# First feed-forward layer of an attention stack: second map in three fp32r passes on split operands, squares of the context rows on GpSimd, their sums spread out

## What is computed

```python
x = x + L0_xattn(layernorm(x), ctx_768, ...)
x = x + L0_ffn(layernorm(x), Wp, sim_matrix, temperature, W1, b1, W2, b2)
x = x + L1_xattn(layernorm(x), ctx_768, ...)
# L0_ffn: E = 8 experts, D = 128, F = 512
comb = top-2 gates of each token, zero for the other experts
h   = gelu(einsum('bsd,edf->ebsf', x, W1) + b1[:, None, None, :])
eo  = einsum('ebsf,efd->ebsd', h, W2) + b2[:, None, None, :]
out = einsum('ebsd,bse->bsd', eo, comb)
```

## Time and profile before

| what | value |
|---|---|
| profiled execution, span | 3638.8 us |
| median of three runs | 3643.95 us |
| PE busy | 97% |
| ACT busy | 71% |
| DVE busy | 51% |
| POOL busy | 24% |

### The profile page before, as it was taken

How to read it: one execution, slowest core, us unless ns; L and a number is a source line. 1 busy time by engine, 2 the same in 40 slices (tenths; PEclk the granted TensorE clock), 3 DMA queues, 4 the chain that set the end, 5 groups by cost and what they waited for, 6 DMA issues and landing times.

```text
span 3638.8 us, 73817 instructions
## 1 busy us (share of the span) xinstructions
PE 3543.7 (97%) x27546; PEld 1564.5 (43%) x27549; DVE 1858.4 (51%) x1946; ACT 2584.6 (71%) x2742; POOL 857.8 (24%) x1977
## 2 busy tenths in 40 slices
PE   7999999999999999999999999999999999999999
PEld 4333333335544444444444444443222222355654
DVE  4222222224287878797888888763321211155445
ACT  6999999995455555555555555549999999944442
POOL 1222222222222323222322222103332223210000
PEclk9999999999999999999999999999999999999999
DMA  6224232211201111111111111000000000020000
GB/s 201 95 80 111 81 102 83 101 67 53 77 30 40 41 40 41 41 40 41 36 44 36 42 39 41 17 23 6 4 4 4 4 6 27 2 71 14 1 1 6
DMA packets 102892, 163.15 MB, mean 45 GB/s; under 512 B 22452, under 2 KB 43344, under 8 KB 101040
## 3 DMA queue, kind: packets, MB, share of 16 engines
q1 hardware_dynamic: 102576, 158.69, 13.5%
HBM read 93.50 MB, written 65.14 MB: 44 GB/s over the span
## 4 chain that ended last, share of the span: by engine, by line
PE 77%; ACT 13%; issue 6%; DVE 2%; ACTq 1%; DMA 0%; SPq 0%; POOL 0%; DVEq 0%; POOLq 0%
PE ps L1109 20%; PE ps L1083 17%; PE ps L748 11%; ACT probs L1532 8%; ACT probs L1543 5%; PE ps L680 4%; PE ps L570 3%; PE ps L576 3%; PE ps L967 3%; PE ps L1298 2%; PE ps L949 2%; PE ps L1408 1%; PE ps L1425 1%; PE ps L1402 1%; PE ps L1281 1%
## 5 line engine op out<-in xcount | busy, mean ns | idle before, releaser
L1694 ACT ACTIVATE probs<-ps 128x1024 f32<-128x1024 f32 x808 | 783.7, 1023 | 577.1 <-PE ps L1083 309.4
L1543 ACT ACTIVATE probs<-ps 128x1024 f32<-128x1024 f32 x1200 | 1119.7, 1030 | 48.1 <-PE ps L680 41.0
L2715 DVE TENSOR_TENSOR vbuf<-vbuf,probs 128x1024 f32<-128x1024 f32 x784 | 1003.3, 1322 | 204.9 <-ACT probs L1694 201.4
L748 PE MATMUL ps<-probs,vst 128*32 128x512 f32 x6400 | 843.8, 598 | 27.1 <-ACT probs L1543 24.4
L1109 PE MATMUL ps<-probs,klo 128*64 128x512 f32 x1888 | 431.0, 599 | 0.0
L2458 DVE COPY qs<-ps 128x512 f32<-128x512 f32 (+1 forms) x208 | 142.2, 684 | 562.9 <-PE ps L576 279.7
L1932 POOL CAST kst<-kb 128x128 fp32r<-128x128 f32 (+1 forms) x800 | 252.8, 316 | 740.4 <-PE ps L748 593.6
L1532 ACT ACTIVATE probs<-ps 128x1536 f32<-128x1536 f32 x268 | 362.1, 1622 | 3.4 <-PE ps L728 1.8
L1109 PE MATMUL ps<-probs,qs 128*64 128x512 f32 x1376 | 313.7, 599 | 0.0
L1944 POOL COPY vst<-vbuf 128x36 f32<-128x36 f32 (+1 forms) x816 | 193.7, 237 | 438.6 <-PE ps L748 432.1
L2049 POOL CAST keys_b<-keys_a 128x512 fp32r<-128x512 f32 (+1 forms) x90 | 108.7, 1207 | 791.1 <-DMA klo<-kv_scratch 529.1
(11 more groups left out here) (505 smaller groups left out, 4044.9 us busy)
## 6 DMA issues: line engine op xcount, KB each, us to landing
kv_scratch<-qs SPq DMA_DIRECT2D x192, 256.0 KB, 2.0
keys_a<-kv_scratch SPq DMA_DIRECT2D x96, 256.0 KB, 2.6
klo<-kv_scratch SPq DMA_DIRECT2D x56, 256.0 KB, 2.9
qs<-kv_scratch SPq DMA_DIRECT2D x40, 256.0 KB, 2.9
kb<-k_scratch SPq DMA_DIRECT2D x12, 816.0 KB, 6.8
vbuf<-in_L_ffn_W SPq DMA_DIRECT2D x16, 256.0 KB, 3.0
kb<-in_L_ffn_W SPq DMA_DIRECT2D x16, 256.0 KB, 3.0
qz<-q_scratch SPq DMA_DIRECT2D x56, 64.0 KB, 2.1
```

What stands on the lines that cost most here:

```text
L748: mm = pe.matmul(ps[band, 6 + half, :], vst[:, r, band], probs[:, r, j * HT:(j + 1) * HT], start=start, stop=stop)
L1543: act.activation(probs[:, r, b * T:(b + 1) * T].rearrange("p (h n) -> p h n", h=2), ps[:, 2 * buf:2 * buf + 2, :], ACT.Exp, scale=HD8 ** - ...
L1694: act.activation(pr1[:, u % BUF1], ps[:, 2 * b:2 * b + 2, :], ACT.Exp, scale=HD64 ** -0.5)\
L2715: dve.tensor_tensor(sum1[:, odd, h], sum1[:, odd, h], e, ALU.add).then_inc(s["added"], 1)
```

## The change

The second map of this layer is made in the way of the first. `W2` is split by GpSimd (cast and subtraction, behind those of `W1`) into `w2_high` and `w2_low`, the low part in the weight's own place. The hidden block is split into `hid_high` and `hid_low` (in place): the casts of blocks 0 and 1 on VectorE, those of blocks 2 and 3 on ScalarE behind its four gelus, all four subtractions on VectorE. TensorE's `second0` goes block by block: four matmuls with the high part of the tokens (both weights, both halves), then a wait for the low part (`hid_rest`) and two with it; `weight8` follows blocks 0 and 2. The f32 matmuls of L967 stay for the other expert layer (m = 1) only.

`context_lengths` is taken apart. The squares go to GpSimd, in four pieces (17, 17 and 16 tiles, and the last four rows), each behind the weight parts of experts 1, 2, 3 and 4. The sums stay on VectorE, a piece each behind experts 2, 3, 4 and 5. The synchronous queue's wait for `piece_used` goes.

```diff
@@ places
+        w2_low = [parts_at[0][:, u * 2 * F + F:(u + 1) * 2 * F] for u in range(2)]
+        w2_high = [parts_at[0][:, 6 * F + 2 * T + u * F:6 * F + 2 * T + (u + 1) * F] for u in range(2)]
+        hid_parts = over("hid_parts", "probs", [P, RING * 4 * HT], F32R)
+        hid_low = hid_parts[:, 0:NF * T].rearrange("p (f h n) -> p f h n", f=NF, h=2)
...
@@ tensor
+                    if m == 0:
+                        return second0(e, u)
...
+                def second0(e, u):
+                    pe.wait_ge(s["eo_used"], e + 1)
+                    pe.wait_ge(s["w2_parts"], since("w2_parts", 2 * e + 2))
+                    for f in range(NF):
+                        name = "hid_first" if f < 2 else "hid_last"
+                        pe.wait_ge(s[name], since(name, 2 * e + f % 2 + 1))
+                        for weights in (w2_high, w2_low):
+                            for h in range(2):
+                                pe.matmul(ps[:, 4 + h, :], weights[u][:, f * D:(f + 1) * D], hid_high[f][:, h, :],
+                                          start=(f == 0 and weights is w2_high), stop=False)
+                        pe.wait_ge(s["hid_rest"], since("hid_rest", e * NF + f + 1))
+                        for h in range(2):
+                            mm = pe.matmul(ps[:, 4 + h, :], w2_high[u][:, f * D:(f + 1) * D], hid_low[:, f, h, :],
+                                           start=False, stop=(f == NF - 1))
+                        if f in (0, 2):
+                            if e == 0 and f == 0:
+                                pe.wait_ge(s["w_copied"], 3)
+                            weight8(e, u, f // 2)
                     mm.then_inc(s["eo_ready"], 1)
@@ scalar, behind the four gelus of an expert
+                    if m == 0:
+                        for f in range(2, NF):
+                            act.wait_ge(s["hid_ready"], n * NF + f + 3)
+                            act.activation(hid_high[f], hid[:, f, :, :], ACT.Copy).then_inc(s["hid_last"], 1)
@@ gpsimd
+            def context_squares(k):
+
+                pool.wait_ge(s["in_piece"], 16 * (kstores[2] + 4))
+                part = cn3[0:TAIL, SF, :] if k == len(PIECES) else cn3[:, PIECES[k][0]:PIECES[k][1], :]
+                pool.tensor_tensor(part, part, part, ALU.mult).then_inc(s["squared"], 1)
...
+                    if m == 0:
+                        second = vbuf[:, u * 2 * F + F:(u + 1) * 2 * F]
+                        pool.tensor_copy(w2_high[u], second).then_inc(s["w2_parts"], 1)
+                        pool.wait_ge(s["w2_parts"], since("w2_parts", 2 * e + 1))
+                        pool.tensor_tensor(w2_low[u], second, w2_high[u].bitcast(F32), ALU.subtract).then_inc(s["w2_parts"], 1)
+                        if 0 <= e - 1 <= len(PIECES):
+                            context_squares(e - 1)
@@ vector
+            def context_lengths(k):
+
+                dve.wait_ge(s["squared"], k + 1)
+                if k == len(PIECES):
+                    then(dve.reduce_sum(lens[0:TAIL, SF:ST], cn3[0:TAIL, SF, :], AX.X))
+                    dve.reduce_max(cpeak[:, 0:1], lens, AX.X).then_inc(s["piece_used"], 1)
+                else:
+                    t0, end = PIECES[k]
+                    if k == 0:
+                        then(dve.memset(lens, 0.0))
+                    then(dve.reduce_sum(lens[:, t0:end], cn3[:, t0:end, :], AX.X))
...
+            def hidden_parts(e):
+
+                for f in range(NF):
+                    dve.wait_ge(s["hid_ready"], e * NF + f + 3)
+                    if f < 2:
+                        dve.tensor_copy(hid_high[f], hid[:, f, :, :]).then_inc(s["hid_first"], 1)
+                    name = "hid_first" if f < 2 else "hid_last"
+                    dve.wait_ge(s[name], since(name, 2 * e + f % 2 + 1))
+                    dve.tensor_tensor(hid_low[:, f, :, :], hid[:, f, :, :], hid_high[f].bitcast(F32), ALU.subtract)\
+                        .then_inc(s["hid_rest"], 1)
...
+                        if m == 0:
+                            hidden_parts(e)
...
-                        if n == 0:
-                            context_lengths()
+                        if m == 0 and 0 <= e - 2 <= len(PIECES):
+                            context_lengths(e - 2)
@@ sync
                     if m == 0 and e == 2:
-                        sp.wait_ge(s["piece_used"], 1)
                         for k in range(NKV):
                             sp.wait_ge(s[f"kv_st{k}"], 16 * (2 * NP * KVST[k] + 1))
```

More of the change, by code:

```diff
@@ L268, in build_program @@
         w_high = [[place[:, 4 * F + u * F:4 * F + (u + 1) * F] for u in range(2)] for place in parts_at]
+        w2_low = [parts_at[0][:, u * 2 * F + F:(u + 1) * 2 * F] for u in range(2)]
+        w2_high = [parts_at[0][:, 6 * F + 2 * T + u * F:6 * F + 2 * T + (u + 1) * F] for u in range(2)]
+        hid_parts = over("hid_parts", "probs", [P, RING * 4 * HT], F32R)
+        hid_more = over("hid_more", "kb", [P, 2 * SP], F32R)
+        hid_low = hid_parts[:, 0:NF * T].rearrange("p (f h n) -> p f h n", f=NF, h=2)
+        hid_high = [place.rearrange("p (h n) -> p h n", h=2) for place in
+                    (hid_parts[:, NF * T:NF * T + T], hid_parts[:, NF * T + T:NF * T + 2 * T],
+                     hid_more[:, 5 * T:6 * T], hid_more[:, 6 * T:7 * T])]
         z_high, z_low = ([place[:, at:at + T].rearrange("p (h n) -> p h n", h=2) for place in parts_at] for at in (6 * F, 6 * F + T))
@@ L316, in build_program @@
                   "gram_ready gram_copied b1_q b1_copied b1_r b1_prod b1_sum b1_max "
-                  "part_high part_rest part_kept w1_parts z_parts k1_parts ").split()
+                  "part_high part_rest part_kept w1_parts z_parts k1_parts squared ").split()
         names += [f"kv_in{k}" for k in range(NLOAD)] + [f"kv_st{k}" for k in range(NKV)]
@@ L322, in build_program, with since @@
         s = {n: sem(n) for n in names}
+        begun_at = {"hid_first": 16, "hid_last": 16, "hid_rest": 32, "w2_parts": 16 * 6}
+        s.update({n: s[first] for n, first in (("hid_first", "in_x"), ("hid_last", "in_ctx0"), ("hid_rest", "in_ctx1"), ("w2_parts", "in_nat"))})
+        def since(name, count):
+            return begun_at[name] + count
         def mode_of(engine, layer):
@@ L983, in expert @@
                                 mm.then_inc(s["sum_ready"], 1)
+                    mm.then_inc(s["eo_ready"], 1)
+                def second0(e, u):
[16 more added lines that the diff above has]
+                            weight8(e, u, f // 2)
                     mm.then_inc(s["eo_ready"], 1)
@@ L2261, in turn_weights @@
                 dve.tensor_copy(wT[:, 5, 0:E8], ps[:, 1, E16:E16 + E8]).then_inc(s["w_copied"], 1)
[L2263 to L2272, removed]
+            lens = cst[:, 0, 0:ST]
+            def context_lengths(k):
[8 more added lines that the diff above has]
+                    then(dve.reduce_sum(lens[:, t0:end], cn3[:, t0:end, :], AX.X))
             def context_mean():
```

## The result

The changed kernel took 3659.88 us (median of five runs, 3655.25 to 3661.21) beside 3643.95 for the kernel before (five runs as well): 1.0042 times as long, with a 95% interval of 1.0029 to 1.0054. The change costs 16 us.

A forecast was written before the change was run, and what follows sets the result against it. The prediction took TensorE to bound the layer, with VectorE and GpSimd holding each other up after the change. Its terms, from the start through expert 7, summed to +12.9 us: span 3651.7, time about 3657, range 3638 to 3666.

The forecast's parts named there:

- TensorE's pace: Second map as fp32r passes: an expert left to itself takes 11.74 us, a gain of 1.22 an expert, 9.8 over eight.
- The start: Ahead of expert 0: the first square on GpSimd holds VectorE's L2659 on the chain until 876.4, +3.6 us.
- The clock rival: New idle ahead of expert 0 and in expert 2 may lower the clock; three places more give 3662; chance 0.10.
- Expert 0: VectorE's casts stand behind gate steps, so TensorE waits 3.2 us for the first high part; +2.7 us.
- Experts 1 and 6: Low parts pushed later in expert 1, TensorE just fed: 11.9 us, -1.1; expert 6: 12.3 us, -0.7.
- The turns: VectorE and GpSimd instructions wait until the other's is over: 0.33 us for a cast, 1.00 for a 512-column subtraction.
- Expert 2: A GpSimd square holds block 2's low part to 15.7, wanted at 12.2, besides smaller waits: 17.9 us, +5.0.
- Experts 3 to 5: VectorE's sums delay the first cast and GpSimd's parts come between: 14.1 us, +1.1 each, +3.3.
- Expert 7 and the tail: GpSimd's key parts now fall into expert 7: 13.1 us, +0.1.
- The one-way rival: GpSimd alone waits for VectorE, so only expert 0's late start counts: -5.3 us, time 3638.6; chance 0.13.
- the rival of long squares that let go between pieces: No 3.6 us at the start, expert 2 falls to 12.3: +3.7 us, time 3647.7; chance 0.10.
- All is hidden: All added work hides behind TensorE, expert 0's too: -9.8 + 0.9 us for the start, time 3635; chance 0.04.

The follow-up runs named there:

- map_alone_w2_later: map_alone, with GpSimd from expert 2 on splitting W2 only when VectorE has made the running expert's low parts; 3642.15 us, 0.9988 times the kernel before.
- first_square_waits: The changed kernel, with GpSimd's first square waiting for VectorE's product ahead of the routing; 3656.58 us, 1.0033 times the kernel before.
- w2_later_full: The changed kernel, with GpSimd from expert 2 on splitting W2 only after VectorE's low parts of the running expert; 3655.40 us, 1.0030 times the kernel before.
- all_moved: The whole change with squares, sums, W2 and key splits and gate steps rearranged, TensorE's low parts a block later; 3637.25 us, 0.9979 times the kernel before.
- squares_alone: The changed kernel with the second map left as f32 matmuls, only squares and sums moved; 3646.17 us, 1.0008 times the kernel before.
- parts_before_shares: The changed kernel with expert 0's high and low parts of blocks 0 and 1 ahead of the gate steps on VectorE; 3659.17 us, 1.0037 times the kernel before.
- all_moved_old_order: all_moved with TensorE block by block and expert 0's gate steps ahead of its second high part; 3641.85 us, 0.9991 times the kernel before.
- map_alone: The changed kernel without squares and sums, a constant standing for the largest squared length; 3646.89 us, 1.0005 times the kernel before.

## Why the prediction was right, and where not

The sign and the mechanism (TensorE waits for VectorE, which waits for GpSimd's instructions) held, and the sum came near: +12.9 forecast, 14.3 measured in the layer, 16 in the medians. That it came so near is in part luck, since errors of up to 5 us in the steps cancel. By steps:

- **TensorE's pace.** Held: 11.74 us an expert with operands in time, 11.69 measured in map_alone_w2_later.
- **The start.** Forecast +3.6 by the product waiting until 876.4. Measured 3.93 us for L2729, so 2.7 of waiting; the square was mis-sized (2.90 us, not 4.05, against 1.27 for a subtraction of 512). But the first map starts at 882.49 (L964), and started at 877.71 (L949) before: +4.8, since the small matmuls then ran at the low clock. The clock rival came in beside the forecast, not in its place; the sum left it out, and here it is 2 us, and about 2 more in expert 0.
- **Expert 0.** Forecast +2.7, measured +4.6 from the first map's start (20.7 for 16.1). The wait for the first high part is there, from L970's end at 891.95 to 895.30 (3.3 us, forecast 3.2); the rest is the low clock: first_square_waits has the same wait with the clock at full speed behind it, and takes 18.9, which is +2.8.
- **Experts 1 and 6.** Forecast 11.9 and 12.3, measured 12.39 and 12.72. The turns were slightly undersized.
- **Expert 2.** Forecast 17.9, measured 12.76: the step that failed. By the walk a square of 3.8 us gets its turn ahead of two low parts. The square was issued when the walk had it, 10.8 us into the expert (926.32); it was VectorE that was further on: the low part of block 1 ended at 8.1, not 10.8, and the last one had been issued at 9.6, so the square came behind them all. In three other runs it was issued at 9.5 to 9.6 and did catch the last one, and then cost 2.5 us with its true length. Here 5 us of forecast loss did not come. Only one execution of the changed kernel was profiled, so whether its other runs went the short way isn't known.
- **Experts 3 to 5.** Forecast 14.1, measured 14.6, 14.6 and 14.3; the step held. The sums, not the squares, do it: expert 5 has no square and takes 14.34, expert 6 has neither and takes 12.72. By w2_later_full, turns with GpSimd's W2 parts are about half of the excess over TensorE's pace.
- **Expert 7 and the tail.** Forecast +0.1, measured +0.9, and the last addition 1.85 us in place of 1.22, beside GpSimd's keys.

So the error of expert 2 (5.1 us too much) was covered by the start and expert 0 (3.1 too little: some 4 of low clock, less the 0.8 by which the square was oversized), the longer turns (1.2 over experts 3 to 5, 0.9 in 1 and 6) and expert 7 with the tail (1.4). The forecast was nearer than its parts. The 5.15 us that I put outside the span are 1.75 for this program by the profiled run of the changed kernel (3657.65 for a span of 3655.9) and about 1.9 in later runs of the kernel before; the rest is how far the profiled execution of before lay below its median, and carries no part of the change.

The one-way rival is out: VectorE waited in L2729, and in every L2610 above 1.22 us, and two runs with equal work differ by 0.66 us an expert through the order of GpSimd's instructions. So is the rival of long squares that let go between pieces: L2729 was issued 0.06 us behind the square and ended at 876.87, 1.09 us behind the square's end, so nearly all of its own 1.22 us came after the square. The Trainium skill (SBUF — State Buffer, section Who interferes with whom) has both directions: it says that a VectorE instruction with two SBUF inputs contends with a GpSimd instruction that reads SBUF, and that issue order decides who blocks. The trace agrees: the square issued first made L2729 take 3.93 us, and in first_square_waits the square, issued at 875.18 after VectorE's next instruction, took 3.82 us instead of 2.90. "All is hidden" is out for the change as it stood; with the order changed, experts 2 to 7 of all_moved are nearly there.

## What to carry to other kernels

GpSimd was idle for most of the layer, and work moved to it was still not free, because its instructions and those of VectorE, which now feeds TensorE, hold each other up: before moving a step, look what the longest instruction of the neighbour is and whose turn it takes. When two moves are tried together, try each alone: here they cost 0 and 2 us alone and 14 together. 4.5 us of the difference are one move's instructions pushing the other's square in front of a product on the chain, and 6.4 fall in the three experts with a sum, in which VectorE had become the late engine. And a helper's work has a place as well as a length: three waits, a few moved calls and another order of TensorE's matmuls turned +0.4% into -0.2% with the same arithmetic.

## Not expected of the hardware

- A GpSimd product of a tile with itself took 2.90 us for 1632 elements and 2.75 for 1536 (squares_alone, undisturbed), so 1.8 ns an element; a subtraction of two tiles of 512 took 1.27, which is 2.5.
- Over 875 to 893 us the granted clock's mean was 0.72 (10 us at the low level) in three of the four kernels in which the square held the product ahead of the routing, and 0.81 in the fourth (parts_before_shares). It was 0.91 (3.2 us) in the kernel before, squares_alone, first_square_waits and all_moved_old_order, but 0.85 in map_alone and 0.81 in map_alone_w2_later and all_moved, where nothing held the product. So the longest low stretch (10 us) stands only behind a wait of TensorE of 3.5 to 3.6 us ahead of the routing matmuls, which is 0.9 us in the kernel before, but that wait doesn't always bring it; what sets the middle values is open.
- Expert 2 took 12.76 us in the changed kernel and 15.2 to 15.3 in three kernels whose text for that expert's VectorE and GpSimd work is the same: by the rows it goes with which engine's instruction is issued first at its start, by 0.1 us or less in two of the three.
